# First cross attention of a decoder: another order of the short halves, of the turn and of the output copy, and the maxima split before they are turned

## The chip, the cores and the metric

The kernel runs on one core of a Trainium2 chip. The metric is the device time of one execution in microseconds; 706.71 us is the median of three runs of the kernel before (704.28 to 708.05).

## What is computed

A decoder of two layers over 4 sequences of 256 tokens with 128 channels: attention, cross attention to a context of 1601 tokens with 64 channels, a mixture of experts, a recurrent layer, a second cross attention and a feed-forward block, each with a residual and a layer norm. The change touches the first cross attention alone, which is a causal self attention and an attention to the context with the same 16 heads, added:

```python
def _xattn(x, cross_input):            # T=256, H=16 heads of D=8, scale 1/sqrt(8); 4 sequences
    q, k, v = heads(x @ Wq + bq), heads(x @ Wk + bk), heads(x @ Wv + bv)
    att = where(causal, einsum('bhqd,bhkd->bhqk', q, k) * scale, -inf)
    y = einsum('bhqk,bhkd->bhqd', softmax(att), v)
    qc = heads(x @ Wcq + bcq)
    kc, vc = heads(cross_input @ Wck + bck), heads(cross_input @ Wcv + bcv)
    attc = einsum('bhqd,bhkd->bhqk', qc, kc) * scale          # 1601 keys
    y = y + einsum('bhqk,bhkd->bhqd', softmax(attc), vc)
    return y @ Wp + bp
x = layernorm(x + attn(x)); x = layernorm(x + _xattn(x, ctx_512)); ...
```

The softmax is taken with the true maximum of each row subtracted.

## The kernel before

The first cross attention is cut into NU = 16 units, one for each sequence and group of four heads. The heads of a group lie as two pairs, e = 0 and 1, in rows 0 to 63 and 64 to 127 of TensorE's array; a pair holds heads j = 0 and 1. Queries and keys are split into three bf16 parts stacked over 48 rows, so that one bf16 product gives the scores to fp32 precision. Each unit is worked on twice:

- *Halves* (`score_part`, L692, and `reduce_half`, L1076) find the row maxima. A unit has HALVES = 15 of them: 12 of 512 keys (i = 0 to 11, VectorE reduces 2 x 512 columns, L1083), one with the last 65 keys of four query tiles (i = 12, L1085), and two for the self attention with its mask (i = 13 of 128 keys and i = 14 of 256, L1090). A half is written to two PSUM banks (`s1`), and there are two such pairs of banks, used in turn: a writer waits in `wait_s1_free` (L317) until what stood there two places earlier in the list `s1_order` has been read.
- After the last half `combine` (L1094) makes the negated maxima `nm` (128 x 16, fp32). TensorE turns them (`turn_maxima`, L723) to 16 rows of 128, in the place of `s1_order` between half 0 and half 1 of the next unit. VectorE's `row` (L1099) copies them to bf16 and subtracts the copy from the fp32 rows for the second part. SyncE then writes the two parts (`max_rows`, L374 to L381) as two more rows under the queries in `qq`, so that the second score product has its maximum subtracted. It is awaited as `max_in` before the first score product of that unit.
- *Score steps* (`scores_t`, L729): a unit has NST = 15, t = 0 to 12 for the context (128 keys each) and 13 and 14 for the self attention. Each gives four products (e, j) with the keys on the partitions; ScalarE takes exponentials of 512 columns for each e (L962), and `outputs` (L748) multiplies them with the values two steps later, into one bank `o_ps`. After a unit's last product ScalarE copies that bank to `o_all` (`copy_out`, L948), and the first product of the next unit waits for the copy. The scores `s2` have three banks (S2_RING), the exponentials four buffers (P_RING).

`scores_and_half` (L776) puts one score step and one half together in TensorE's queue, and the halves run S1_LEAD + HALVES = 22 steps ahead of the scores. So step g of the loop works on half (g + 22) mod 15 of a unit one or two ahead. 22 halves stand before the loop, in the start-up, and the last 22 score steps have no half beside them. Order and waits are written out by hand for every engine; semaphores count, and an engine's queue is strictly in order.

In TensorE's queue a step is: scores (0,0), half e = 1, scores (0,1), scores (1,0), half e = 0, scores (1,1), then, where i = 0, the turn, and then the four value products of the step before the last. Halves are counted by position i in the queue; VectorE follows in the same order. In ScalarE's queue the output copy of unit n - 1 stands behind both exponentials of step t = 1 of unit n.

## Time and profile before

| | us |
|---|---|
| median of 3 runs | 706.71 |
| lowest, highest | 704.28, 708.05 |
| the profiled execution | 703.72 |
| its span | 701.9 |
| PE, VectorE, ScalarE, GpSimd busy | 620.9, 527.3, 451.0, 205.6 |

The page gives shares and groups of one execution. The loop of the first cross attention runs from about 84 to 395 us of the span; an output copy (L950) marks every unit, the first at 108.7 and the last at 389.1. Times in the timelines are from the span's start. An entry such as "x8" merges eight instructions in a row, and its duration runs from the first's start to the last's end.

### The profile page before, as it was taken

How to read it: one execution, taken by the hardware profiler on the slowest of the kernel's cores; microseconds unless marked ns; L12 is line 12 of the kernel's file. 1: busy time of each engine (PE TensorE's matmuls, PEld its weight loads, DVE VectorE, ACT ScalarE, POOL GpSimd, SP SyncE). 2: the span in 40 equal slices, each digit the busy share in tenths (PEclk: the TensorE clock that was granted, in tenths of full speed). 3: DMA queues.
4: the chain of work that ended last, by engine and by line, in shares of the span. 5: the costliest groups of instructions: out<-in, count | busy, mean ns of one | idle time of the engine just before them, and what ended most of it. 6: DMA issues, size and time to landing. Idle time of an engine off the chain costs nothing. (4 is left out here: it accounts for less than half of the span.)

```text
span 701.9 us, 13641 instructions
## 1 busy us (share of the span) xinstructions
PE 620.9 (88%) x5206; PEld 341.4 (49%) x5207; DVE 527.3 (75%) x706; ACT 451.0 (64%) x814; POOL 205.6 (29%) x277
## 2 busy tenths in 40 slices
PE   8989899999999999999999796998709999978996
PEld 5645433333334333333433375886205556646883
DVE  5369889999999999999945464999298557868432
ACT  3555578888898888888887432655771056566223
POOL 7224532344455577766740030000000000005000
PEclk9999989999999999999999978999968999999998
DMA  8258575555565554544210287451000010000000
GB/s 204 95 148 267 172 227 173 140 116 138 161 157 121 124 138 98 116 96 97 66 36 1 70 299 312 151 166 59 0 2 0 0 46 1 1 1 1 0 1 30
DMA packets 43293, 70.74 MB, mean 101 GB/s; under 512 B 12492, under 2 KB 31652, under 8 KB 42720
## 3 DMA queue, kind: packets, MB, share of 16 engines
q1 hardware_dynamic: 31696, 38.34, 21.0%
q0 software_dynamic: 10928, 29.32, 13.5%
q10 hardware_dynamic: 608, 2.25, 1.4%
q8 instruction: 40, 0.66, 0.4%
q14 instruction: 21, 0.17, 0.1%
HBM read 44.41 MB, written 24.79 MB: 99 GB/s over the span
## 5 line engine op out<-in xcount | busy, mean ns | idle before, releaser
L962 ACT ACTIVATE prob<-ps 128x512 f32<-128x512 f32 (+2 forms) x480 | 253.1, 582 | 45.9 <-PE ps L738 38.8
L1083 DVE TENSOR_REDUCE pm<-ps 128x2 f32<-128x1024 f32 x192 | 225.8, 1215 | 6.6 <-PE ps L700 4.8
L761 PE MATMUL ps<-prob,vst 128*9 128x256 f32 (+1 forms) x1664 | 129.8, 384 | 10.2 <-ACT o_all L950 10.2
L738 PE MATMUL ps<-qq,kc 50*128 50x256 bf16 (+1 forms) x832 | 134.3, 275 | 0.1
L700 PE MATMUL ps<-kc,qq 48*128 48x512 bf16 x384 | 116.4, 388 | 2.9 <-DVE pm L1083 2.6
L738 PEld LDWEIGHTS ps<-qq,kc 50*128 50x128 bf16 (+1 forms) x832 | 52.1, 96 | 94.0 <-ACT prob L962 69.3
L761 PEld LDWEIGHTS ps<-prob,vst 128*9 128x9 f32 (+1 forms) x1664 | 25.1, 88 | 51.7 <-ACT prob L962 39.1
L1635 POOL DMA_DIRECT2D w_w<-in_w x2 | 1.1, 534 | 148.1 <-PE ps L1672 148.1
L1090 DVE TENSOR_REDUCE nm<-ps 128x4 f32<-128x512 f32 (+1 forms) x32 | 30.6, 958 | 14.9 <-PE ps L688 14.9
L700 PEld LDWEIGHTS ps<-kc,qq 48*128 48x128 bf16 x384 | 32.9, 93 | 13.2 <-DVE pm L1083 9.4
L688 PE MATMUL ps<-masks_b 64*128 64x256 bf16 x256 | 37.6, 269 | 0.0
L1663 PE MATMUL ps<-w_wgate 128*128 128x384 f32 x54 | 21.2, 540 | 17.2 <-DVE r_sn L2073 17.2
L1315 PE MATMUL ps<-x_high,up_high 128*128 128x512 f32 x64 | 26.6, 415 | 10.3 <-DVE hv L1483 6.4
L1394 ACT ACTIVATE sg<-ps,exp_bias 128x512 f32<-128x512 f32 x32 | 21.9, 685 | 17.3 <-PE ps L1317 17.2
L1399 ACT ACTIVATE hh_high<-whole 128x512 fp32r<-128x512 f32 x32 | 20.1, 627 | 19.7 <-DVE whole L1491 19.7
L1483 DVE SCALAR_TENSOR_TENSOR hv<-ps,exp_bias,sg 128x512 f32<-128x512 f32 x32 | 23.9, 746 | 9.5 <-DMA comb_bc<-comb_scr 7.5
L518 POOL TENSOR_TENSOR o_all<-o_all,below 128x512 f32<-128x512 f32 x13 | 16.5, 1271 | 48.4 <-DMA below<-rden_scr 48.4
L1989 ACT ACTIVATE ctx_t<-ps,base 128x512 f32<-128x512 f32 x16 | 11.0, 688 | 29.8 <-PE ps L1750 29.8
L1934 ACT ACTIVATE ps<-shift 128x512 f32<-128x512 f32 (+1 forms) x28 | 15.7, 569 | 21.4 <-DVE shift L2171 18.9
L1640 POOL TENSOR_TENSOR ctx<-ctx_t,ctx 128x512 fp32r<-128x512 f32 x4 | 5.2, 1292 | 72.9 <-DVE ctx L2230 72.9
L1317 PE MATMUL ps<-x_high,up_low 128*128 128x512 f32 x64 | 26.2, 410 | 0.0
L1316 PE MATMUL ps<-x_low,up_high 128*128 128x512 f32 x64 | 26.1, 408 | 0.0
(362 smaller groups left out, 1292.3 us busy)
## 6 DMA issues: line engine op xcount, KB each, us to landing
kc<-kc_scr SPq DMA_DIRECT2D x32, 300.2 KB, 5.0
comb_bc<-comb_scr SPq DMA_DIRECT2D x7, 512.0 KB, 4.7
below<-rden_scr POOLq DMA_DIRECT2D x13, 256.0 KB, 6.0
ctx<-ctx_scr POOLq DMA_DIRECT2D x1, 3204.0 KB, 15.0
raw<-in_wexp POOLq DMA_DIRECT2D x8, 384.0 KB, 3.9
exp_scr<-raw_high POOLq DMA_DIRECT2D x8, 384.0 KB, 3.5
exp_scr<-raw_low POOLq DMA_DIRECT2D x8, 384.0 KB, 4.4
kc_scr<-hi SPq DMA_DIRECT2D x6, 400.2 KB, 4.8
```

The costliest lines, as they stand in the source:

```text
L688: done = pe.matmul(o, ident_b[rows, half, :], mask[rows, half, :].unsqueeze(1).to_broadcast([64, 2, 128]), start=False, stop=(half == 1), ...
L700: return pe.matmul(bank, qq[s][rows, 0, j, t * 128:(t + 1) * 128], kc[s][rows, j, c * 512:(c + 1) * 512], start=True, stop=True)
L738: last = pe.matmul(bank[0:p, j * TQ:(j + 1) * TQ], kc[s][rows, j, t * 128:t * 128 + p], qq[s][rows, 0, j, :], start=(j == 0), stop=True, s ...
L761: last = pe.matmul(o_ps[32 * hh:32 * hh + VW, kind * TQ + q0:(kind + 1) * TQ], value[:, hh * VW:(hh + 1) * VW], prob[0:k, (NST * n + t) % ...
L962: act.activation(prob[0:p, g % P_RING, 2 * e:2 * e + 2, q0:TQ], s2[0:p, k % S2_RING, 0:2 * w].rearrange("p (i q) -> p i q", i=2), ACT.Exp, ...
L1083: dve.tensor_reduce(pm[:, m % 2, c, :, jt], banks, AX.X, ALU.max).then_inc(s1_read, 1)
L1090: dve.tensor_reduce(nm[:, :, 1, :].rearrange("p e (j t) -> p e j t", t=2)[:, :, :, t], banks[:, :, 0:2 * w].rearrange("p e (j n) -> p e j ...
L1315: pe.matmul(o, weight[0], x[0], start=start, stop=False, skip_group_check=True)
L1316: pe.matmul(o, weight[0], x[1], start=False, stop=False, skip_group_check=True)
L1317: return pe.matmul(o, weight[1], x[0], start=False, stop=True, skip_group_check=True)
L1394: act.activation(sg[:, k % 2, :], ps[:, k % 2, :], ACT.Silu, bias=exp_bias[s][:, f:f + 1]).then_inc(sg_done, 1)
L1483: dve.scalar_tensor_tensor(out=hv[:, k % 2, :], in0=ps[:, 2 + k % 2, :], scalar=exp_bias[s][:, NF + f:NF + f + 1], in1=sg[:, k % 2, :], op ...
```

## The change

- A table HALF_AT gives for each position in a unit which half is worked on there. From unit 2 on the order is 0, 1, 2, 12, 3, 4, 5, 13, 6, 7, 8, 14, 9, 10, 11; units 0 and 1 keep the old one. The wait for the self-attention queries goes with half 13.
- `turn_maxima` moves from the end of the step of half 0 into the step of half 1, behind both score products of e = 0 and ahead of the half. Its place in `s1_order` stays.
- The maxima are split on VectorE at once in `combine`: a cast of 128 x 16 to bf16 and a subtract, into `nm_parts`. The turn is then two bf16 matrix products with the identity, each 16 x 128, side by side in one bank. `row` leaves VectorE; ScalarE copies 16 x 256 in one instruction, behind both exponentials of the step of half 1.
- `copy_out` stands behind the first exponential of t = 1 and not behind the second.

```diff
@@ -51,6 +51,12 @@
 QPART = (0, 1, 2, 0, 1, 0)
 SLOTS = 4
 HALVES, TURN = 15, -1
+HALF_AT = (0, 1, 2, 12, 3, 4, 5, 13, 6, 7, 8, 14, 9, 10, 11)
+
+
+def half_at(m, i):
+    return HALF_AT[i] if m >= 2 else i
+
 P_RING, S2_RING = 4, 3
 S1_LEAD = 7
 WARM = 7
@@ -204,6 +210,7 @@
             vss = held(st, "vss", [128, NB, NG, 2, 4 * VW])
             pm = held(st, "pm", [128, 2, 4, 2, 4])
             nm = held(st, "nm", [128, 2, 2, 4])
+            nm_parts = held(st, "nm_parts", [128, 2, 16], BF16)
             mrow = [held(st, f"mrow{s}", [16, 2, 128], BF16) for s in range(SLOTS)]
             ps = st.enter_context(nc.psum_tensor("ps1", [128, 8, 512], F32))
             s1 = ps[:, 4:8, :].rearrange("p (n e) k -> p n e k", e=2)
@@ -691,7 +698,7 @@
 
                     def score_part(m, i, e):
 
-                        s, n = m % SLOTS, s1_at[m, i]
+                        s, n, i = m % SLOTS, s1_at[m, i], half_at(m, i)
                         bank = s1[:, n % 2, e, :]
                         rows = head_rows(e)
                         if i < 12:
@@ -716,7 +723,7 @@
                     def score_wait(m, i):
                         if i == 0:
                             pe.wait_ge(slot_in[m % SLOTS], SLOT_INC * (m // SLOTS + 1))
-                        if i == 13:
+                        if half_at(m, i) == 13:
                             pe.wait_ge(self_in[m % SLOTS], SELF_INC * (m // SLOTS + 1))
                         wait_s1_free(pe, s1_at[m, i])
 
@@ -724,7 +731,10 @@
                         n = s1_at[m, TURN]
                         wait_s1_free(pe, n)
                         pe.wait_ge(nm_ready, m + 1)
-                        pe.transpose(s1[0:16, n % 2, 0, 0:128], nm[:].rearrange("p e k i -> p (e k i)"), ident).then_inc(s1_ready, 1)
+                        for part in range(2):
+                            last = pe.matmul(s1[0:16, n % 2, 0, part * 128:(part + 1) * 128], nm_parts[:, part, :], ident_b[:, 0, :],
+                                             start=(part == 0), stop=True, skip_group_check=True)
+                        last.then_inc(s1_ready, 1)
 
                     def scores_t(n, t, e, j):
 
@@ -767,11 +777,11 @@
                     def half(h):
 
                         m, i = h // HALVES, h % HALVES
+                        if i == 1 and m:
+                            turn_maxima(m - 1)
                         score_wait(m, i)
                         score_part(m, i, 1)
                         score_part(m, i, 0).then_inc(s1_ready, 1)
-                        if i == 0 and m:
-                            turn_maxima(m - 1)
 
                     def scores_and_half(g, h):
 
@@ -781,18 +791,18 @@
                         m, i = h // HALVES, h % HALVES
                         more = m < NU
                         scores_t(n, t, 0, 0)
+                        if i == 1 and m <= NU:
+                            scores_t(n, t, 0, 1)
+                            turn_maxima(m - 1)
                         if more:
                             score_wait(m, i)
                             score_part(m, i, 1)
-                        scores_t(n, t, 0, 1)
+                        if i != 1 or m > NU:
+                            scores_t(n, t, 0, 1)
                         scores_t(n, t, 1, 0)
                         if more:
                             score_part(m, i, 0).then_inc(s1_ready, 1)
                         scores_t(n, t, 1, 1)
-                        if more and i == 0:
-                            turn_maxima(m - 1)
-                        if h == NU * HALVES:
-                            turn_maxima(NU - 1)
 
                     pe.wait_ge(masks_cast, 1)
                     for h in range(HALVES + S1_LEAD):
@@ -935,6 +945,12 @@
                     for j in range(5, LATE_KEYS):
                         middle(j - 1)
                         high(j)
+                    def row(m):
+                        n = s1_at[m, TURN]
+                        act.wait_ge(s1_ready, n + 1)
+                        act.activation(mrow[m % SLOTS][:].rearrange("p i n -> p (i n)"), s1[0:16, n % 2, 0, 0:256],
+                                       ACT.Copy).then_inc(mrow_ready, 1)
+
                     for h in range(HALVES + S1_LEAD):
                         if h == 0:
                             middle(LATE_KEYS - 1)
@@ -944,6 +960,8 @@
                             high(late_keys[h])
                         if h in late_values:
                             values(late_values[h])
+                        if h == HALVES + 1:
+                            row(0)
 
                     def copy_out(n):
                         act.wait_ge(av_done, NST * (n + 1))
@@ -962,8 +980,11 @@
                             act.activation(prob[0:p, g % P_RING, 2 * e:2 * e + 2, q0:TQ],
                                            s2[0:p, k % S2_RING, 0:2 * w].rearrange("p (i q) -> p i q", i=2),
                                            ACT.Exp, scale=SCALE).then_inc(exp_done, 1)
-                            if t == 1 and e == 1 and n:
+                            if t == 1 and e == 0 and n:
                                 copy_out(n - 1)
+                        m, i = divmod(g + HALVES + S1_LEAD, HALVES)
+                        if i == 1 and m <= NU:
+                            row(m - 1)
                     copy_out(NU - 1)
                     act_ln2a(0)
                     act_ln2a_v(0)
@@ -1075,7 +1096,7 @@
                         values(5 + i)
                     def reduce_half(m, i):
 
-                        n = s1_at[m, i]
+                        n, i = s1_at[m, i], half_at(m, i)
                         dve.wait_ge(s1_ready, n + 1)
                         banks = s1[:, n % 2, :, :]
                         if i < 12:
@@ -1094,15 +1115,14 @@
                     def combine(m):
                         dve.wait_ge(s1_read, HALVES * (m + 1))
                         dve.tensor_reduce(nm[:, :, 0, :], pm[:, m % 2].rearrange("p c e i -> p e i c"), AX.X, ALU.max,
-                                          negate=True).then_inc(nm_ready, 1)
-
-                    def row(m):
-                        n, u = s1_at[m, TURN], m % SLOTS
-                        dve.wait_ge(s1_ready, n + 1)
-                        dve.tensor_copy(mrow[u][:, 0, :], s1[0:16, n % 2, 0, 0:128]).then_inc(m1_done, 1)
-                        dve.wait_ge(m1_done, m + 1)
-                        dve.tensor_tensor(mrow[u][:, 1, :], s1[0:16, n % 2, 0, 0:128], mrow[u][:, 0, :],
-                                          ALU.subtract).then_inc(mrow_ready, 1)
+                                          negate=True).then_inc(m1_done, 1)
+                        whole = nm[:].rearrange("p e k i -> p (e k i)")
+                        dve.wait_ge(m1_done, 2 * m + 1)
+                        if m:
+                            dve.wait_ge(mrow_ready, m)
+                        dve.tensor_copy(nm_parts[:, 0, :], whole).then_inc(m1_done, 1)
+                        dve.wait_ge(m1_done, 2 * m + 2)
+                        dve.tensor_tensor(nm_parts[:, 1, :], whole, nm_parts[:, 0, :], ALU.subtract).then_inc(nm_ready, 1)
 
                     def reciprocals(n):
                         at = slice(n % 2 * DEN, (n % 2 + 1) * DEN)
@@ -1129,8 +1149,6 @@
                     for m in range(NU):
                         for i in range(HALVES):
                             reduce_half(m, i)
-                            if m and i == 0:
-                                row(m - 1)
                             if m >= 3 and i == 8:
                                 reciprocals(m - 3)
                             if m * HALVES + i in late_keys:
@@ -1139,7 +1157,6 @@
                                 dve.wait_ge(v_act, len(values_order) - DVE_VALUES)
                                 dve.memset(o_ps, 0.0).then_inc(o_zero, 1)
                         combine(m)
-                    row(NU - 1)
                     last_normalise(NU - 3)
                     projected(0)
                     last_normalise(NU - 2)
```

TensorE's queue around the turn of unit 1 (`nm`), before; `ps1` holds all banks, `qq0,kc0` are the score products of unit 0, `kc2,qq2` the halves of unit 2, `prob,vst` the value products:

```order
L738 MATMUL ps1<-qq0,kc0 128x256 [waits exp_done]
L700 MATMUL ps1<-kc2,qq2 128x512
L738 MATMUL ps1<-qq0,kc0 128x256
L727 MATMUL ps1<-base,nm 16x128 [waits nm_ready,s1_read]
L761 MATMUL ps1<-prob,vst 9x256 [waits exp_done]
L761 MATMUL ps1<-prob,vst 9x256 x3
L738 MATMUL ps1<-qq0,kc0 128x256 [waits exp_done]
L700 MATMUL ps1<-kc2,qq2 128x512 [waits s1_read]
L738 MATMUL ps1<-qq0,kc0 128x256
L738 MATMUL ps1<-qq0,kc0 128x256 [waits exp_done]
```

The same place in the changed kernel:

```order
L771 MATMUL ps1<-prob,vst 9x256 [waits exp_done]
L771 MATMUL ps1<-prob,vst 9x256 x3
L748 MATMUL ps1<-qq0,kc0 128x256 [waits exp_done]
L748 MATMUL ps1<-qq0,kc0 128x256
L735 MATMUL ps1<-masks_b,nm_parts 16x128 [waits nm_ready,s1_read]
L735 MATMUL ps1<-masks_b,nm_parts 16x128
L707 MATMUL ps1<-kc2,qq2 128x512 [waits s1_read]
L748 MATMUL ps1<-qq0,kc0 128x256 [waits exp_done]
L707 MATMUL ps1<-kc2,qq2 128x512
L748 MATMUL ps1<-qq0,kc0 128x256
L771 MATMUL ps1<-prob,vst 9x256 [waits exp_done]
L771 MATMUL ps1<-prob,vst 9x256 x3
```

The turn now stands between the score products of e = 0 and the half, one step later, and the score products of e = 1 stand behind the half.

VectorE's queue around it, before, from the short halves at the end of a unit to the rows' cast and subtract:

```order
L1085 TENSOR_REDUCE pm<-ps1 128x8 [waits s1_ready]
L1090 TENSOR_REDUCE nm<-ps1 128x2x2 [waits s1_ready] x2
L1096 TENSOR_REDUCE nm<-pm 128x2x4 [waits s1_read]
L1083 TENSOR_REDUCE pm<-ps1 128x2 [waits s1_ready]
L1102 CAST mrow1<-ps1 16x128 [waits s1_ready]
L1104 TENSOR_TENSOR mrow1<-ps1,mrow1 16x128 [waits m1_done]
```

and in the changed kernel:

```order
L1111 TENSOR_REDUCE nm<-ps1 128x2x2 [waits s1_ready]
L1104 TENSOR_REDUCE pm<-ps1 128x2 [waits s1_ready] x3
L1117 TENSOR_REDUCE nm<-pm 128x2x4 [waits s1_read]
L1123 CAST nm_parts<-nm 128x16 [waits mrow_ready,m1_done]
L1125 TENSOR_TENSOR nm_parts<-nm,nm_parts 128x16 [waits m1_done]
L1104 TENSOR_REDUCE pm<-ps1 128x2 [waits s1_ready] x3
```

The cast and the subtract have moved from behind the first reduction (L1083) of the next unit to ahead of it, and the masked half (L1090, now L1111) lies three plain reductions before the end.

ScalarE's queue at the step of half 1 in the changed kernel, where the kernel before has exponentials alone, and then at t = 1 of a unit, before and after:

```order
L980 ACTIVATE prob<-ps1 128x512 [waits s2_ready]
L980 ACTIVATE prob<-ps1 128x512 [waits s2_ready,av_done]
L980 ACTIVATE prob<-ps1 128x512 [waits s2_ready]
L951 ACTIVATE mrow3<-ps1 16x256 [waits s1_ready]
L980 ACTIVATE prob<-ps1 128x512 [waits s2_ready,av_done]
```

```order
L962 ACTIVATE prob<-ps1 128x512 [waits s2_ready]
L962 ACTIVATE prob<-ps1 128x512 [waits s2_ready,av_done]
L962 ACTIVATE prob<-ps1 128x512 [waits s2_ready]
L950 ACTIVATE o_all<-ps1 128x512 [waits av_done]
L962 ACTIVATE prob<-ps1 128x512 [waits s2_ready,av_done]
L962 ACTIVATE prob<-ps1 128x512 [waits s2_ready]
```

```order
L980 ACTIVATE prob<-ps1 128x512 [waits s2_ready]
L980 ACTIVATE prob<-ps1 128x512 [waits s2_ready,av_done]
L968 ACTIVATE o_all<-ps1 128x512 [waits av_done]
L980 ACTIVATE prob<-ps1 128x512 [waits s2_ready]
L980 ACTIVATE prob<-ps1 128x512 [waits s2_ready,av_done]
```

The row copy (L951) stands behind the exponentials of its step, and the output copy (L950, now L968) passes one exponential.

## Rows read from the trace of the kernel before

**Rows 1.** The page: span, busy, two groups (busy, mean ns | idle before).

```profile
span 701.9 us, 13641 instructions
...
PE 620.9 (88%) x5206; PEld 341.4 (49%) x5207; DVE 527.3 (75%) x706; ACT 451.0 (64%) x814; POOL 205.6 (29%) x277
...
L962 ACT ACTIVATE prob<-ps 128x512 f32<-128x512 f32 (+2 forms) x480 | 253.1, 582 | 45.9 <-PE ps L738 38.8
L1083 DVE TENSOR_REDUCE pm<-ps 128x2 f32<-128x1024 f32 x192 | 225.8, 1215 | 6.6 <-PE ps L700 4.8
```

**Rows 2.** Windows: stretch, us, busy time of each engine, clock, DMA share, GB/s.

```profile
202.00:221.00 19.00, 17.63 (x240) 7.22 (x237) 17.62 (x20) 16.56 (x33) 10.20 (x14) 1.00 0.62 149
```

**Rows 3.** Timeline, ScalarE: start, us, engine, line, operation [idle before <-releaser].

```profile
202.14 0.61 ACT L950 ACTIVATE o_all<-ps 128x512 f32<-128x512 f32 x1
...
211.84 4.35 ACT L962 ACTIVATE prob<-ps 128x512 f32<-128x512 f32 x8 [1.12 <-PE ps L738]
...
220.80 0.61 ACT L950 ACTIVATE o_all<-ps 128x512 f32<-128x512 f32 x1
```

**Rows 4.** Timeline, VectorE, around the end of a unit's halves.

```profile
207.38 0.69 DVE L1090 TENSOR_REDUCE nm<-ps 128x4 f32<-128x512 f32 x1 [0.34 <-PE ps L688]
208.70 1.23 DVE L1090 TENSOR_REDUCE nm<-ps 128x4 f32<-128x1024 f32 x1 [0.62 <-PE ps L688]
209.96 0.21 DVE L1096 TENSOR_REDUCE nm<-pm 128x8 f32<-128x32 f32 x1
210.08 1.22 DVE L1083 TENSOR_REDUCE pm<-ps 128x2 f32<-128x1024 f32 x1
211.21 0.27 DVE L1102 CAST mrow<-ps 16x128 bf16<-16x128 f32 x1
211.51 0.28 DVE L1104 TENSOR_TENSOR mrow<-ps,mrow 16x128 bf16<-16x128 f32 x1
211.90 9.39 DVE L1083 TENSOR_REDUCE pm<-ps 128x2 f32<-128x1024 f32 x8
```

**Rows 5.** TensorE: steps, turn, halves 1 and 2, awaited product.

```profile
207.83 0.28 PE L738 MATMUL ps<-qq,kc 50*128 50x256 bf16 x1
...
209.14 0.28 PE L738 MATMUL ps<-qq,kc 50*128 50x256 bf16 x1
...
210.31 0.27 PE L727 MATMUL ps<-base,nm 128*16 128x128 f32 x1 [0.56 <-DVE nm L1096]
...
211.35 0.39 PE L700 MATMUL ps<-kc,qq 48*128 48x512 bf16 x1
...
212.44 0.39 PE L700 MATMUL ps<-kc,qq 48*128 48x512 bf16 x1
...
213.53 0.28 PE L738 MATMUL ps<-qq,kc 50*128 50x256 bf16 x1
...
218.24 0.28 PE L738 MATMUL ps<-qq,kc 50*128 50x256 bf16 x1
...
221.55 0.62 PE L761 MATMUL ps<-prob,vst 128*9 128x256 f32 x8 [0.68 <-ACT o_all L950]
```

**Rows 6.** Waits, window 110 to 370: who waited for whom: us, times, longest.

```profile
PEld ps L727 <- DVE nm L1090: 11.5, 14, 1.0
PE ps L761 <- ACT o_all L950: 9.5, 14, 0.7
```

**Rows 7.** SyncE timeline, and GB/s over 211 to 218 us.

```profile
211.82 2.74 SPq L380 DMA_DIRECT2D qq<-mrow  x4
...
GB/s 94 94 54 7 0 0 0 0 0 0 0 0 12 0 0 0 12 0 0 0 12 0 0 0 12 0 220 203 256 73 183 366 335 237 79 116 262 116 146 329
```

**Rows 8.** Timelines, small operations on ScalarE and VectorE.

```profile
79.96 0.52 ACT L898 ACTIVATE vst<-ps 128x432 f32<-128x432 f32 x1
80.34 0.22 DVE L1004 TENSOR_TENSOR rem<-ps,hi 128x65 f32<-128x65 f32 x1
83.92 0.29 ACT L898 ACTIVATE vst<-ps 65x144 f32<-65x144 f32 x1 [0.18 <-PE ps L582]
```

## The prediction

> **What bounds the kernel now.** I read the page first: TensorE (PE) is busy 88% of the span and the two costliest groups are ScalarE's exponentials (L962) and VectorE's maxima (L1083) [rows 1]. Busy shares don't name a limit here, so I took the table of windows. In one stretch of 19.00 us in the middle of the cross attention PE is busy 17.63, VectorE 17.62 and ScalarE 16.56 [rows 2]: three engines within 1.1 us of each other, at the full clock. What counts is then the waits that they pass on to one another, and I read the timeline of each engine over one unit.
>
> The output copy (L950), once in each unit, gives the period: it starts at 202.14 and 220.80 [rows 3], 18.66 us for 15 steps. A step without anything special takes PE 1.09 us (212.44 to 213.53) [rows 5], ScalarE 1.09 (8 exponentials in 4.35 us, two to a step) [rows 3] and VectorE about 1.17 (8 reductions in 9.39) [rows 4]. 15 plain steps of 1.09 would be 16.35, so 2.3 us of the period are extras: mask steps (the step from 207.83 to 209.14 takes 1.31 [rows 5], there are four, one of them with a shorter product behind it), the turn of the maxima, and the wait of the first product of a unit for the output copy, 0.68 at 221.55 [rows 5], 9.5 us over 14 units [rows 6].
>
> The turn is the largest. VectorE starts its last reduction of a unit at 208.70 and ends at 209.93. Call this end R. It combines (209.96, 0.21), reduces the first half of the next unit (210.08, 1.22, end 211.30), then casts and subtracts the turned rows (211.21, 211.51; they are ready at 211.79) [rows 4]. PE turns at 210.31, starts half 1 of the next unit at 211.35, as soon as half 0 has been read (R + 1.42), and half 2 at 212.44 (R + 2.51) [rows 5]. ScalarE is idle 1.12 us before 211.84 for it [rows 3], and PE's weight load for the turn waits 11.5 us over 14 units [rows 6].
>
> **The change, part by part.**
>
> *The turn and the split.* Halves and the turn share two buffers in turn. Order: half 0, turn, half 1, half 2. So half 1 waits until half 0 has been read, and half 2 until the turned rows have been copied. Neither rule is changed, but what stands ahead of both gets longer.
>
> Step one, VectorE. The combine is followed by a cast and a subtract of 128x16, each waiting for the one before. The trace has no such operation. The nearest are the combine, 0.21 for 32 elements to 8 [rows 4], and a subtract of 65 columns from PSUM, 0.22 [rows 8]; the ends are 0.10 and the 0.28 of the subtract of 128 columns [rows 4]. I take 0.18 each, a little under the 65-column one. With the 0.03 us between dependent ones (209.93 to 209.96, 211.48 to 211.51) and the 0.09 by which an independent reduction starts ahead of its predecessor's end (210.08 against 210.17) the reduction of half 0 starts at R + 0.03 + 0.21 + 2 x (0.03 + 0.18) - 0.09 = R + 0.57 and ends at R + 1.79; it ended at R + 1.37. PE gets to half 1 at R + 1.84, 0.42 later than now.
>
> Step two, PE. Before, the wait for the maxima stood behind all score products of step 0. Now the turn stands inside step 1, ahead of half 1, and the scores of the second head pair (e = 1) stand behind half 1's first part. They can't start before R + 1.84. From the start of half 1's first part to their results is 0.23 + 0.11 + 0.27 = 0.61 us (the product L738 is 0.28 long [rows 5]; the other two are half a half's columns and one product's columns, as the 1.09-step spaces them). The exponential starts at about R + 2.49.
>
> Step three, ScalarE. The row copy stands behind that exponential, so it starts one exponential later (4.35 / 8 = 0.54): R + 3.03. Its price: the copies of 144 and 432 columns took 0.29 and 0.52 [rows 8], so 256 columns are near 0.38, with these two as ends. Rows ready at R + 3.41, half 2 on PE at R + 3.45 instead of R + 2.51: **+0.94 us** per unit. With 0.10 or 0.28 for the two split operations it is +0.78 or +1.14. The two casts from PSUM that VectorE loses (0.27 + 0.28) [rows 4] give nothing back, since they ran while VectorE waited for half 1 anyway (211.35 + 0.55 = 211.90).
>
> The Trainium skill (VectorE: DVE Perf Modes, "The TRN2 errata") gives two prices that differ for the small operations: 58 + FD cycles for SBUF to SBUF, which would be 0.08 us, and (N + 151)/0.96 ns for an fp32 tensor_tensor, 0.17 us. By the first the turn would cost +0.74 instead of +0.94, by the second it stays. This trace shows nothing under 0.2 us on VectorE [rows 4, 8], so it leans to the second.
>
> *Short steps.* A 4 x 65-column half and the two self-attention halves move from the end of the unit to places 3, 7 and 11, for all units but the first two. Instructions and durations stay. The last half is then a plain one. Start of step to start of reduction was 0.87 for the masked one (207.83 to 208.70) and is 0.55 for a plain one (211.35 to 211.90) [rows 4, 5]: -0.32. The mask step's extra of 1.31 - 1.09 = 0.22 now lies ahead of it: +0.22. Together **-0.10**. That VectorE no longer idles through three short halves in a row is worth nothing as long as PE and ScalarE set the pace between turns, and with 1.09 against their 1.09 they do.
>
> *Output copy.* It is queued one exponential earlier, so the first product's wait of 0.68 [rows 5] shrinks by 0.54, at most. The exponential it passes is later by the copy's own place in the queue (0.61 long [rows 3]), and the product behind needs that one. Gain between 0 and 0.54; I take the middle, **-0.30**.
>
> *Knock-on.* ScalarE has 0.3 us more work per unit and enters half 2 with two waits (before e = 1 and before the next step) in place of one. It is busy 16.56 of 19.00 [rows 2], so it can catch up, but only at PE's pace. 0 to 0.3, I take **+0.15**.
>
> Sum: 0.94 - 0.10 - 0.30 + 0.15 = **+0.69 us** per unit, the ends 0.78 - 0.10 - 0.54 = +0.14 and 1.14 - 0.10 + 0.3 = +1.34. It is paid where a turn is followed by halves of the next unit in the steady loop: turns 1 to 14, so 14 x 0.69 = +9.7 (ends +2 and +19). Turn 0 lies in the start-up, turn 15 has no half behind it; the last unit wins the copy's 0.3. These cancel. The profiled execution is at 703.7 (span 701.9 [rows 1] and 1.8 around it), 3 us below the median of 706.7; the sum is put on the median: 716.5.
>
> **The rivals.**
>
> *The rows reach the next unit too late.* SyncE issues four small transfers in 2.74 us from 211.82 [rows 7] and the next unit's first scores start at 218.24 [rows 5], 6.45 us after the rows were ready. The rows are now ready at R + 3.41 instead of R + 1.86, 1.55 later, and everything behind is 0.94 later: 5.8 us are left. The line of bytes over 211 to 218 us shows four equal pulses of 12 GB/s, the last one 24 slices of 0.175 us in, at 215.2 [rows 7]: 3.4 to 3.6 us after the rows. So some 2 us of margin. If loads of experts or of keys fall on these transfers (the same line stands at 200 and more right behind them) and it takes 7 us, each unit pays 1.2 more: 716.5 + 14 x 1.2 = 733. Chance 0.08, and half of that price in some units is likelier than all of it.
> The Trainium skill (DMA: Bandwidth & Descriptors, the table of fixed and variable cost) says some 2.0 us for one transfer; behind three issues of about 0.7 that makes 4.1 us, inside the 5.8 as well.
>
> *Faster: VectorE's queue was the bound.* The change was then worth what VectorE idles now. Its own work after it would be 12 plain halves x 1.17, two of 128 and 65 columns at 0.69 less the 0.08 of overlap, 1.20 for the longer masked one and 0.57 for combine and split [rows 4]: 14.04 + 1.22 + 1.20 + 0.57 = 17.0 us, and 0.55 for the one half that nothing covers (between half 0 and half 1 VectorE has no rows to split any more): 17.6 per unit, 1.1 below 18.66, and 706.7 - 15 = 692. It decides if, at the turn, half 0 has been read before PE comes to half 1. For it: three short halves in a row now leave VectorE idle, and spread out they let it catch up, since 1.17 against 1.09 means that it falls behind in long rows. Against it: the chain R to half 2 is made of waits that the order of the code forces, however early R is, and moving R earlier by an idle time of VectorE needs PE to deliver earlier. Chance 0.14, with anything from 692 to 703.
>
> *No difference.* The chain is at its low end and the copy's gain at its high end: +0.14 x 14 = +2, 703 to 710. Chance 0.12.
>
> **How the numbers follow.** Forecast (711 to 723, likeliest 716.5) 0.66, late rows 0.08, same 0.12, faster 0.14. A measurement of this kernel can tell about 0.5%, 3.5 us, from no change. Slower by more: 0.66 + 0.08 = 0.74; within: 0.12; faster: 0.14. The range leaves out the faster case and the top of the late one: 703 to 724.
>
> **What would show it.** In the profile of the changed kernel: the output copies 19.3 us apart in place of 18.66; before one exponential in each unit an idle time of ScalarE above 1 us with a second one behind it; PE's first half product waiting for VectorE's maxima once in a unit, and once for ScalarE's row copy, which did not exist; the wait of the first value product for the output copy near 0.15. If the copies are 17.6 apart and PE waits for neither, step two is wrong. If the first scores of a unit wait for the rows' transfer, the first rival holds. If the split operations take 0.1 each or less, the size is wrong, by 0.2 us per unit.

## The result, and the profile after

The changed kernel takes 728.7 us, the median of four runs (722.8 to 734.0), against 705.5 us for the kernel before beside it: a ratio of 1.031, 95% interval 1.026 to 1.037. It was forecast slower, 716.5 with a range to 724, so the sign was right and the size was not: +23 us in place of +10. One of the four executions, 722.8, lies inside the range. Executions more than 1.5% above the fastest of the same kernel, here 734.0, are left out of every ratio but not out of the medians. The profiled execution took 729.7, with a span of 727.9.

The page of the changed kernel, the lines that answer to [rows 1]; PEclk is the granted clock in 40 slices, in tenths:

```profile
span 727.9 us, 13704 instructions
...
PE 643.0 (88%) x5222; PEld 344.3 (47%) x5223; DVE 528.5 (73%) x706; ACT 455.0 (63%) x830; POOL 205.7 (28%) x277
...
PEclk9999789989999999999999998899967999999999
...
L980 ACT ACTIVATE prob<-ps 128x512 f32<-128x512 f32 (+2 forms) x480 | 252.2, 584 | 63.0 <-PE ps L748 55.1
L1104 DVE TENSOR_REDUCE pm<-ps 128x2 f32<-128x1024 f32 x192 | 230.2, 1218 | 37.1 <-PE ps L707 35.9
```

The busy times of VectorE and ScalarE have hardly moved, but VectorE's idle time ahead of its reductions went from 6.6 to 37.1 us and ScalarE's ahead of its exponentials from 45.9 to 63.0. TensorE (PE) is busy 22 us longer with 16 instructions more: something made the same products take longer.

The output copies mark the units. In ScalarE's timeline of the changed kernel four of them stand here:

```profile
175.47 0.60 ACT L968 ACTIVATE o_all<-ps 128x512 f32<-128x512 f32 x1
...
194.79 0.60 ACT L968 ACTIVATE o_all<-ps 128x512 f32<-128x512 f32 x1
...
215.57 0.60 ACT L968 ACTIVATE o_all<-ps 128x512 f32<-128x512 f32 x1
...
236.39 0.60 ACT L968 ACTIVATE o_all<-ps 128x512 f32<-128x512 f32 x1
```

They are 19.32, 20.78 and 20.82 us apart, where [rows 3] had 18.66. Of the first 13 distances six lie between 19.32 and 19.57 and seven between 20.78 and 22.24. The kernel before has 18.66 to 18.78 for all 13. So there are two losses, one in every unit and one in about half of them.

**The first loss is the chain of the turn.** VectorE's timeline in the changed kernel around one turn:

```profile
220.08 3.48 DVE L1104 TENSOR_REDUCE pm<-ps 128x2 f32<-128x1024 f32 x3
223.59 0.21 DVE L1117 TENSOR_REDUCE nm<-pm 128x8 f32<-128x32 f32 x1
223.83 0.17 DVE L1123 CAST nm_parts<-nm 128x16 bf16<-128x16 f32 x1
224.04 0.17 DVE L1125 TENSOR_TENSOR nm_parts<-nm,nm_parts 128x16 bf16<-128x16 f32 x1
224.13 1.22 DVE L1104 TENSOR_REDUCE pm<-ps 128x2 f32<-128x1024 f32 x1
```

ScalarE's at the same turn:

```profile
226.05 0.60 ACT L980 ACTIVATE prob<-ps 128x512 f32<-128x512 f32 x1 [1.22 <-PE ps L748]
226.55 0.36 ACT L951 ACTIVATE mrow<-ps 16x256 bf16<-16x256 f32 x1
227.62 1.08 ACT L980 ACTIVATE prob<-ps 128x512 f32<-128x512 f32 x2 [0.71 <-PE ps L748]
```

And TensorE's:

```profile
223.76 0.39 PE L748 MATMUL ps<-qq,kc 50*128 50x256 bf16 x2
224.36 0.27 PE L735 MATMUL ps<-masks_b,nm_parts 128*16 128x128 bf16 x2 [0.22 <-DVE nm_parts L1125]
225.41 0.39 PE L707 MATMUL ps<-kc,qq 48*128 48x512 bf16 x2 [0.78 <-DVE pm L1104]
...
226.96 0.55 PE L707 MATMUL ps<-kc,qq 48*128 48x512 bf16 x1 [0.18 <-ACT mrow L951]
```

The last reduction of the unit ends at 223.56; this is R. Half 1 starts at R + 1.85, the exponential of e = 1 at R + 2.49 after 1.22 us of idle time, the rows are ready at R + 3.35 and half 2 starts at R + 3.40. In the kernel before it was R + 2.51 [rows 4, 5].

**The second loss is TensorE's clock.** The windows of 2 us behind this turn (stretch, us, busy time of PE, PEld, DVE, ACT, POOL, granted clock, DMA share, GB/s):

```profile
224.00:226.00 2.00, 1.01 (x12) 0.38 (x14) 1.37 (x4) 0.84 (x2) 1.81 (x4) 1.00 0.09 17
226.00:228.00 2.00, 1.82 (x19) 0.54 (x22) 1.41 (x2) 1.24 (x3) 0.00 (x0) 0.76 0.65 197
228.00:230.00 2.00, 2.00 (x26) 0.73 (x20) 1.30 (x2) 1.16 (x3) 1.43 (x2) 0.50 0.02 3
230.00:232.00 2.00, 2.00 (x29) 0.78 (x23) 1.20 (x2) 1.58 (x4) 1.70 (x2) 0.88 0.67 157
```

PE was busy half of the window at the turn. Then the granted clock falls to 0.50, which is 1.2 GHz in place of 2.4, and comes back 3.4 us later (227.0 to 230.5). The windows of the kernel before showed the full clock in mid-loop [rows 2].

The waits of the changed kernel in its loop, 110 to 390 us:

```profile
PE ps L707 <- DVE pm L1104: 10.1, 13, 0.8
...
PE ps L735 <- DVE nm_parts L1125: 4.0, 13, 1.1
...
PE ps L771 <- ACT o_all L968: 3.0, 14, 0.2
PE ps L707 <- ACT mrow L951: 2.2, 12, 0.2
...
PEld ps L748 <- DMA qq<-mrow: 0.4, 1, 0.4
```

The wait for the output copy, 9.5 us in [rows 6], is 3.0; the waits for the row copy are new, those for half 0 go from 0.2 us at the most to 0.8; the rows' transfers made nobody wait but once.

**The books.** From the profile of before (701.9) to that of after (727.9) are 26.0 us. The first output copy stands at 113.1 instead of 108.7: 4.4. The first 13 distances sum to 263.9 against 13 x 18.68 = 242.8: 21.1, of which 13 x (19.33 - 18.68) = 8.5 is the chain and 12.6 stands on top, 12.3 of it in the seven longer units. Not all of that is the clock: in two of the seven a split operation on VectorE was held up, 1.0 us together (see "The clock"). The last two distances gained 0.6, and behind the last copy 1.1 came on top. Which units are hit differs from one to the next and the medians cover several executions, so the 12.6 is this execution's.

### The profile page after: what moved, and what is told of

It is laid out like the page before. It is cut to its first block and busy times, and to the rows that moved or that the text cites. A ratio compares the mean times of both kernels' runs of the same rounds, so it can differ in the third digit from the quotient of the medians.

```text
span 727.9 us, 13704 instructions
## 1 busy us (share of the span) xinstructions
PE 643.0 (88%) x5222; PEld 344.3 (47%) x5223; DVE 528.5 (73%) x706; ACT 455.0 (63%) x830; POOL 205.7 (28%) x277
## 5 line engine op out<-in xcount | busy, mean ns | idle before, releaser
L1104 DVE TENSOR_REDUCE pm<-ps 128x2 f32<-128x1024 f32 x192 | 230.2, 1218 | 37.1 <-PE ps L707 35.9
L748 PE MATMUL ps<-qq,kc 50*128 50x256 bf16 (+1 forms) x832 | 143.1, 283 | 0.4 <-ACT vst L908 0.2
L771 PE MATMUL ps<-prob,vst 128*9 128x256 f32 (+1 forms) x1664 | 136.3, 401 | 3.2 <-ACT o_all L968 3.2
L707 PE MATMUL ps<-kc,qq 48*128 48x512 bf16 x384 | 118.7, 401 | 17.3 <-DVE pm L1104 14.0
L748 PEld LDWEIGHTS ps<-qq,kc 50*128 50x128 bf16 (+1 forms) x832 | 55.1, 97 | 105.4 <-ACT prob L980 75.3
L1416 ACT ACTIVATE hh_high<-whole 128x512 fp32r<-128x512 f32 x32 | 20.1, 627 | 21.5 <-DVE whole L1508 21.5
L1111 DVE TENSOR_REDUCE nm<-ps 128x4 f32<-128x512 f32 (+1 forms) x32 | 30.7, 958 | 2.6 <-PE ps L695 1.4
L1951 ACT ACTIVATE ps<-shift 128x512 f32<-128x512 f32 (+1 forms) x28 | 15.7, 569 | 21.4 <-DVE shift L2188 18.9
L509 POOL DMA_DIRECT2D below<-o_all x13 | 9.2, 707 | 70.1 <-ACT o_all L968 70.1
```

The lines of the kernel that those rows point to most:

```text
L707: return pe.matmul(bank, qq[s][rows, 0, j, t * 128:(t + 1) * 128], kc[s][rows, j, c * 512:(c + 1) * 512], start=True, stop=True)
L748: last = pe.matmul(bank[0:p, j * TQ:(j + 1) * TQ], kc[s][rows, j, t * 128:t * 128 + p], qq[s][rows, 0, j, :], start=(j == 0), stop=True, s ...
L771: last = pe.matmul(o_ps[32 * hh:32 * hh + VW, kind * TQ + q0:(kind + 1) * TQ], value[:, hh * VW:(hh + 1) * VW], prob[0:k, (NST * n + t) % ...
L1104: dve.tensor_reduce(pm[:, m % 2, c, :, jt], banks, AX.X, ALU.max).then_inc(s1_read, 1)
L1111: dve.tensor_reduce(nm[:, :, 1, :].rearrange("p e (j t) -> p e j t", t=2)[:, :, :, t], banks[:, :, 0:2 * w].rearrange("p e (j n) -> p e j ...
```

## The experiments

Each was measured beside the kernel before on the same chip. "At full clock" below is the distance that recurs among the first 13 output copies. The mean granted clock is that of the windows from 114 to 352 us.

### One part at a time

`order_only` is the kernel before with the new places of the short halves, `copy_only` with the earlier output copy, `turn_only` the changed kernel without these two:

```diff
--- order_only against the kernel before (and half_at(m, i) where a half is written and reduced)
+HALF_AT = (0, 1, 2, 12, 3, 4, 5, 13, 6, 7, 8, 14, 9, 10, 11)
--- copy_only against the kernel before
-                            if t == 1 and e == 1 and n:
+                            if t == 1 and e == 0 and n:
--- turn_only against the changed kernel
-HALF_AT = (0, 1, 2, 12, 3, 4, 5, 13, 6, 7, 8, 14, 9, 10, 11)
+HALF_AT = tuple(range(15))
-                            if t == 1 and e == 0 and n:
+                            if t == 1 and e == 1 and n:
```

> The kernel before with the new places of the short halves alone. The two traces say that the turn costs what was lost (output copies 19.33 us apart in the units at full clock, 18.67 before) and that TensorE's clock then falls to half after some of the turns (20.8 apart). Theory A, the turn: the order of halves moves no wait of the turn, so +0 to +0.15 us per unit, 704 to 709. Rival, the order of halves: with plain halves at the end VectorE arrives later at the turn, at least a third of the 22 us comes from it: 713 or more.

> The kernel before with the output copy one exponential earlier, alone. The first value product of a unit waited 0.68 us for it. Theory A: the wait falls to 0.15 to 0.2 and some of it comes back elsewhere, -0.15 to -0.3 us per unit, 701 to 704. Rival: the exponential that it passes is late by as much, no change, 706.

> The changed kernel with the old order of the halves and the old place of the output copy: the split, the bf16 turn inside the step of half 1 and ScalarE's row copy are left. Theory A (turn and clock carry all of the loss, and the copy's own gain of 0.34 us per unit is inside the changed kernel's time): copies 19.4 to 19.7 apart at full clock, half clock after some turns, 727 to 735. Rival (loss comes from the combination with the order of halves): under 722.

| kernel | us | ratio to before (95%) | copies apart at full clock | mean clock |
|---|---|---|---|---|
| order_only | 707.2 | 1.004 (1.001 to 1.006) | 18.78 | 1.00 |
| copy_only | 699.9 | 0.992 (0.989 to 0.995) | 18.33 | 1.00 |
| turn_only | 736.2 | 1.045 (1.039 to 1.051) | 19.56 | 0.94 |
| the change | 728.7 | 1.031 (1.026 to 1.037) | 19.33 | 0.95 |

Against 18.67 the parts are +0.11, -0.34 and +0.89 us per unit. Their sum, +0.66, is the distance of the whole change, 19.33: at full clock the parts add up. The output copy is a gain by itself and the turn is the loss, together with all of the half clock. The rivals of all three expectations fall. Theory A holds for the distances; two times lie outside their ranges, `copy_only` 1.1 us below and `turn_only` 1.2 above.

### The clock

`fill3` gives TensorE three products without use behind the turn, while it waits for half 0 to be read. Nobody reads them.

```diff
                         last.then_inc(s1_ready, 1)
+                        constant = masks_b[:].rearrange("p i h n -> p (i h n)")
+                        for _ in range(3):
+                            pe.matmul(s1[:, n % 2, 1, :], constant[:, 0:128], constant[:, 0:512], start=True, stop=True)
```

> The changed kernel with three matrix products of 512 columns without use behind each turn, written to the bank beside the turned rows, so that TensorE has work while it waits for VectorE to read half 0 (0.78 us in the trace). Theory A, the clock falls because TensorE stands idle at the turn: no unit at half clock, all output copies 19.3 to 19.4 apart, 716 to 719. Rival, the clock falls for another reason (or the idle time is not what decides): 726 to 731, and the copies 20.8 apart as often as now.

Measured: 715.2 us, 1.017 (1.011 to 1.023), 0.8 us below the expected range, and below the changed kernel by 13 us with 48 products more. The window of 114 to 352 us, of the kernel before:

```profile
114.00:352.00 238.00, 222.03 (x3013) 91.72 (x3005) 220.52 (x243) 206.31 (x396) 134.96 (x192) 1.00 0.51 120
```

Of the changed kernel:

```profile
114.00:352.00 238.00, 221.29 (x2794) 86.51 (x2790) 204.78 (x224) 193.57 (x377) 124.78 (x175) 0.95 0.47 117
```

Of `fill3`:

```profile
114.00:352.00 238.00, 226.92 (x2930) 90.28 (x2939) 213.47 (x235) 200.60 (x392) 129.57 (x183) 1.00 0.48 118
```

The mean clock is back at 1.00. Eleven of the 13 distances are 19.32 to 19.37; two are 19.90 and 19.99, at full clock, for a reason of their own (below). The first output copy stands at 108.2, where the kernel before has it, so the 4.4 us of the start-up go away with the filling too. That the clock falls because TensorE stands idle at the turn is shown by this: nothing else was changed, and the chain of 19.33 is untouched. The length of a wait alone doesn't decide: in the start-up of `fill3` TensorE waits 0.88 and 0.94 us in one piece (before 80.5 and 88.7 us), and the clock stays full.

**A third effect: the split is sometimes held up.** This is what lengthened the two units of `fill3`. GpSimd's and VectorE's timelines there:

```profile
134.73 1.81 POOL L480 TENSOR_TENSOR raw_low<-raw,raw_high 128x768 fp32r<-128x768 f32 x1
135.81 0.76 DVE L1126 CAST nm_parts<-nm 128x16 bf16<-128x16 f32 x1
```

The cast takes 0.76 us in place of 0.17 and ends 0.03 us after GpSimd's operation. In the traces of the seven kernels that split the maxima in SBUF, 26 of 224 casts and subtracts take 0.31 to 1.44 us, and each of the 26 ends 0.03 to 0.04 us after a cast or tensor_tensor of GpSimd. In the seven kernels that read the turned rows from PSUM, the same two operations take 0.27 and 0.28 us all 224 times. This is read from the traces; no experiment tested it. The changed kernel has two of the 26 (a subtract of 0.31 and a cast of 1.03), `turn_only` five, `fill3` two, `e1_first` three, `e1_fill` six, `turn_end` and `row_between` four each. In the five kernels without filling all 18 turns with such an operation are followed by half clock, of the 52 other turns of the loop nine.

### Step two: the scores of e = 1 behind the half

`e1_first` sends the score products of e = 1 ahead of half 1 in the step of the turn; `e1_fill` is the same with two products without use ahead of the turn and two ahead of half 1.

```diff
                             scores_t(n, t, 0, 1)
                             turn_maxima(m - 1)
+                            scores_t(n, t, 1, 0)
+                            scores_t(n, t, 1, 1)
                         if more:
                             score_wait(m, i)
                             score_part(m, i, 1)
```

> The changed kernel with the score products of e = 1 ahead of the half in the step of the turn, so that ScalarE's second exponential and the row copy behind it don't wait for VectorE to read half 0. Split, bf16 turn and row copy on ScalarE stay. Theory A (step two of the chain, the scores of e = 1 queued behind the half): rows ready about 1.2 us earlier, half 2 no longer waits for them, 18.6 to 18.9 us per unit, TensorE's idle time shorter and the clock held: 706 to 711. Rival (the split on VectorE and the row copy themselves are the price): 716 or more.

> The run with the score products of e = 1 ahead of the half, and on top two products without use between the slot's release and the turn and two between those scores and half 1. That run had units of 18.65 us at full clock and of 20.4 to 20.6 with half clock. Theory A (idle time at the turn lowers the clock): all units at 18.65 to 18.8, 704 to 708, no difference to the kernel before. Rival: the clock falls as often, 711 to 715.

`e1_first`: 713.4 us, 1.012 (1.005 to 1.020). At full clock the copies are 18.64 to 18.71 apart, one 18.90. That is 0.68 us of each unit back with the split, the bf16 turn and ScalarE's row copy in place. It is the distance of the kernel before, but the other two parts are in it too: 18.67 + 0.11 - 0.34 = 18.44, so of the turn's 0.89 us 0.21 are left. ScalarE's timeline at an ordinary turn, idle 0.15 in place of 1.22 before the exponential in front of the row copy:

```profile
258.24 0.60 ACT L985 ACTIVATE prob<-ps 128x512 f32<-128x512 f32 x1 [0.15 <-PE ps L748]
258.74 0.36 ACT L956 ACTIVATE mrow<-ps 16x256 bf16<-16x256 f32 x1
```

TensorE is idle 0.22 us before that turn and 0.46 before half 1:

```profile
257.61 0.27 PE L735 MATMUL ps<-masks_b,nm_parts 128*16 128x128 bf16 x2 [0.22 <-DVE nm_parts L1130]
...
258.66 0.39 PE L707 MATMUL ps<-kc,qq 48*128 48x512 bf16 x2 [0.46 <-DVE pm L1109]
```

No ordinary turn of the loop, eleven in all, is followed by half clock. The other three are those where GpSimd held the cast up (0.45, 0.55 and 0.62 us long); the first wait is then 0.50 to 0.67, and the three distances are 20.4 to 20.6. One such stretch in the windows:

```profile
198.00:200.00 2.00, 1.27 (x14) 0.45 (x14) 1.51 (x3) 1.21 (x3) 1.71 (x3) 0.99 0.00 0
200.00:202.00 2.00, 2.00 (x22) 0.56 (x14) 1.56 (x2) 0.94 (x2) 1.65 (x4) 0.50 0.11 19
```

So the distance was forecast rightly and the time, 706 to 711, was not: the clock was not held in every unit.

`e1_fill`: 709.6 us, 1.007 (1.004 to 1.010), no unit at half clock (mean clock 1.00), though six split operations are held up. Eight of its copies are 18.9 apart and not 18.65, the five others 19.0 to 19.6: four products are more than the gap holds, and each unit pays 0.27 us for them. So it comes out 1.6 us above the expected range. The traced execution, 714.5, is the slowest of its ten.

### The place of the turn and of the row copy

`turn_end` puts the turn back to the end of the step of half 0 and the row copy behind that step's exponentials. `row_between` leaves the turn and puts the row copy between the two exponentials of its step.

```diff
--- turn_end against the changed kernel (scores_and_half; half and the row copy go with it)
-                        if i == 1 and m <= NU:
-                            scores_t(n, t, 0, 1)
-                            turn_maxima(m - 1)
...
                         scores_t(n, t, 1, 1)
+                        if i == 0 and m <= NU:
+                            turn_maxima(m - 1)
--- row_between against the changed kernel, inside the loop over e
+                            m, i = divmod(g + HALVES + S1_LEAD, HALVES)
+                            if e == 0 and i == 1 and m <= NU:
+                                row(m - 1)
```

> The changed kernel with the turn back at the end of the step of half 0, behind all of its score products, and the row copy behind that step's exponentials. The split on VectorE ahead of half 0's reduction and the copy on ScalarE stay. Theory A: the chain is then 0.4 us longer than before the change (the split) and no longer 0.9, TensorE's idle time is cut in two by the turn: copies 18.8 to 19.0 apart, clock mostly held, 708 to 714. Rival (not the place of the turn but the split and the row copy): 19.3 and more, above 716.

> The changed kernel with ScalarE's row copy between the two exponentials of its step in place of behind them; nothing else. Theory A, step three: the row copy no longer waits for the exponential of e = 1, whose scores stand behind half 1; half 2 waits for the rows no more, copies 18.8 to 18.9 apart at full clock against 19.33. TensorE's idle time of 0.78 us before half 1 stays, and so do the units at half clock: 718 to 723. Rival (the place of the row copy is nothing, the wait for half 0's reduction is all): 19.3 apart, 726 to 731.

`turn_end`: 711.6 us, 1.008 (1.004 to 1.011), copies 18.86 apart at full clock. With the turn where it was, the split and the row copy cost 18.86 - 18.44 = 0.42 us per unit, 18.44 being 18.67 with the two other parts (+0.11 - 0.34), and the other 0.47 of the turn's 0.89 are its new place, with the row copy's. The time lies in the expected range. The traced execution, 721.6, does not stand for it: of eleven executions four, this one among them, took 718 to 723 and seven 706 to 713. In it five of the 13 distances are 20.4 to 22.6, four of them at turns where a split operation was held up. At an ordinary turn TensorE waits longer in one piece than in the changed kernel, and one of ten such turns, not this one, was followed by half clock:

```profile
198.17 0.22 PE L735 MATMUL ps<-masks_b,nm_parts 128*16 128x128 bf16 x1 [1.09 <-DVE nm_parts L1123]
```

`row_between`: 718.8 us, 1.018 (1.011 to 1.024), seven copies 18.86 to 18.94 apart at full clock, one 19.12 and five 20.4 to 22.7, four of these five with a split operation held up. ScalarE's timeline:

```profile
215.32 0.36 ACT L951 ACTIVATE mrow<-ps 16x256 bf16<-16x256 f32 x1
216.64 0.60 ACT L980 ACTIVATE prob<-ps 128x512 f32<-128x512 f32 x1 [0.96 <-PE ps L748]
```

The row copy now runs 1.3 us before the exponential that it used to stand behind, and 19.33 - 18.87 = 0.46 us of each unit are saved by exchanging two entries of one queue. The exponential of e = 1 is as late as ever; only half 2 doesn't wait for it through the row copy. Both expectations of distance are met, and both kernels, whose gaps at the turn were left open, show half clock after five of 14 turns.

### Shortening the chain

If the time of a unit follows the two reductions around the turn, they should be short ones. `best1` is the kernel before with the earlier output copy and halves ordered for that: the 65-column half first, the 128-key half last. `pool_early` is the kernel before with GpSimd's broadcast of the reciprocals issued before its splits; `best2` has both, and `best3` also a later place for VectorE's reciprocals.

```diff
--- best1 against the kernel before (with half_at as above, and the wait for the self-attention data at the first of its two halves)
+HALF_AT = (12, 0, 1, 2, 3, 4, 5, 6, 7, 14, 8, 9, 10, 11, 13)
-                            if t == 1 and e == 1 and n:
+                            if t == 1 and e == 0 and n:
--- pool_early against the kernel before, best2 against best1
                                 gather(n - 2)
+                        if 1 <= n <= POOL_UNITS:
+                            reciprocals_back(n - 1)
...
                                 split_slab(i)
-                        if 1 <= n <= POOL_UNITS:
-                            reciprocals_back(n - 1)
--- best3 against best2
-                            if m >= 3 and i == 8:
+                            if m >= 3 and i == 12:
```

> The kernel before with the output copy one exponential earlier and another order of halves from unit 2 on: the 4 x 65-column half first, the 128-key self half last, the 256-key one in the tenth place; turn, cast and subtract as before. Theory A says that the time of a unit follows the chain of two reductions around the turn (last half, then half 0): with 0.69 in place of 1.23 and 1.22 it is 1.1 us shorter, and VectorE keeps pace between turns: copies 17.5 to 17.8 apart against 18.67, 686 to 692. Rival (the sum of VectorE's work is the bound, whatever the order): 18.2 to 18.3 as with the earlier copy alone, 698 to 701.

> The kernel before with GpSimd issuing the transfer that broadcasts the reciprocals before it splits experts and context, not after. GpSimd waited 48 us for that transfer in the window of the loop, but nothing waits for GpSimd while a unit takes 18.67 us. So no difference: 702 to 706, copies 18.67 apart. It is the control for the next two.

> The last run of the eight before (the 65-column half first, the 128-key half last, earlier output copy), whose copies stood 17.42 us apart but in four units 19 to 24, where VectorE waited up to 3.4 us for the denominators that GpSimd sends; with the broadcast issued before GpSimd's splits. Theory: GpSimd's cycle of 19 to 20 us falls below 17.4, no such wait, all units at 17.4: 686 to 690. Rival: GpSimd is not what is late, 695 to 698.

> As the run before, and VectorE takes the reciprocals behind its thirteenth half of a unit in place of the ninth, 4.4 us later, so that late denominators meet no wait. Theory: if the earlier broadcast alone is enough, the same time as without it, within 2 us; if some denominators are still late, 1 to 4 us less.

| kernel | us | ratio to before (95%) | copies apart |
|---|---|---|---|
| best1 | 696.5 | 0.989 (0.984 to 0.994) | 17.42, four of 17.9 to 23.9 |
| pool_early | 705.2 | 1.000 (0.998 to 1.003) | 18.67 |
| best2 | 686.3 | 0.973 (0.968 to 0.979) | 17.41 to 17.54, all 13 |
| best3 | 687.8 | 0.974 (0.969 to 0.980) | 17.51, one of 19.8 and one of 17.9 |

`best1` came out 0.1 us under its distance, 17.42, and missed its time. Its rival, that VectorE's work is the bound in any order, is refuted by the distance; what was missing is a third party. In two units VectorE waited for the denominators that GpSimd sends, and GpSimd for its own broadcast; VectorE's timeline in `best1`:

```profile
308.29 0.25 DVE L1118 RECIPROCAL below<-below 128x16 f32<-128x16 f32 x1 [3.37 <-DMA below<-o_all]
```

Two lines of its waits, 110 to 370 us:

```profile
POOL o_all L524 <- DMA below<-rden_scr: 60.6, 12, 7.4
...
DVE below L1118 <- DMA below<-o_all: 5.0, 2, 3.4
```

From one transfer of the denominators to the next GpSimd takes 20.0 us on the mean in `best1` between 161 and 321 us, so it falls behind units of 17.42. In the kernel before, three rounds of 19.8 to 21.5 are followed by shorter ones, and VectorE never waited for them. TensorE also waited three times, up to 2.0 us, for the rows' transfer, which is what the prediction's first rival described. In `best2` the first of these waits is

```profile
POOL o_all L524 <- DMA below<-rden_scr: 4.6, 1, 4.6
```

and the second is gone. The same edit alone changes nothing (`pool_early`), as a wait on an engine that nobody waits for should not. VectorE around the turn in `best2`:

```profile
202.39 0.68 DVE L1096 TENSOR_REDUCE nm<-ps 128x4 f32<-128x512 f32 x1
203.10 0.20 DVE L1102 TENSOR_REDUCE nm<-pm 128x8 f32<-128x32 f32 x1
203.32 0.70 DVE L1091 TENSOR_REDUCE pm<-ps 128x8 f32<-128x520 f32 x1
203.94 0.27 DVE L1108 CAST mrow<-ps 16x128 bf16<-16x128 f32 x1
204.24 0.28 DVE L1110 TENSOR_TENSOR mrow<-ps,mrow 16x128 bf16<-16x128 f32 x1
204.85 9.29 DVE L1089 TENSOR_REDUCE pm<-ps 128x2 f32<-128x1024 f32 x8 [0.33 <-PE ps L706]
```

TensorE's at the same turn:

```profile
203.46 0.27 PE L733 MATMUL ps<-base,nm 128*16 128x128 f32 x1 [0.16 <-DVE nm L1102]
...
204.21 0.28 PE L744 MATMUL ps<-qq,kc 50*128 50x256 bf16 x1
...
205.30 0.28 PE L744 MATMUL ps<-qq,kc 50*128 50x256 bf16 x1
```

Here the 0.91 us between 17.42 and `copy_only`'s 18.33 can be counted. TensorE waits 0.16 for the maxima and not 0.56: 0.40. Half 0 has been read when TensorE comes to half 1, so that step takes 1.09 (204.21 to 205.30) and not the 1.38 of `copy_only` (209.54 to 210.92): 0.29. And the wait for the output copy, 0.21 in `copy_only`, is gone. Which of the three moved halves brought how much was not taken apart. `best3` is no better than `best2`. Its units are 17.51 apart, and in the one of 19.8 TensorE waited 1.32 us for the rows' transfer and ran 3.4 us at half clock.

## Why the prediction was wrong

The direction and the chain of the turn were right. The step that failed is the sum: it took the chain's length as the whole price and put TensorE's clock at full, so the half clock behind the turn's waits had no term. The time lay 4.7 us above the range.

- **What bounds the kernel.** Three engines nearly level, so that waits passed on at the turn decide: held. The rival that VectorE's queue is the bound asked for units of 17.6 us and for no wait of TensorE; they took 19.33, with both waits.
- **The split.** 0.18 us for each operation, measured 0.17 where GpSimd doesn't hold it up; half 1 at R + 1.84, measured R + 1.85. That an operation between two SBUF tiles could be held up by GpSimd had no term either: 1.0 us in this trace. Of the two figures in the Trainium skill (VectorE: DVE Perf Modes, "The TRN2 errata") the one for an fp32 tensor_tensor, (N + 151)/0.96 ns, gives 0.174 for 16 columns, and the trace agrees; 58 + FD cycles (the table's 58 + FD/Accel with Accel at 1), 0.08, is half of what was measured.
- **Steps two and three.** Exponential at R + 2.49, measured R + 2.49; row copy 0.38, measured 0.36; half 2 at R + 3.45, measured R + 3.40. The price of the turn, +0.94 per unit, is +0.89 in `turn_only`. `e1_first` and `row_between` show each link apart: 0.68 and 0.46 us come back.
- **Short steps.** -0.10 forecast, +0.11 measured in `order_only`: the wrong sign. The step let a plain last reduction start 0.55 us behind its step on TensorE. In `order_only` VectorE reduces without a pause up to the end of the unit, one start every 1.13 us against TensorE's 1.09, and the last reduction starts 0.77 behind its step (207.20 to 207.97). With 0.22 more, -0.10 becomes +0.12.
- **Output copy.** -0.30 forecast, -0.34 measured in `copy_only`. The wait was to be near 0.15 and is 3.0 / 14 = 0.21.
- **Knock-on.** +0.15 forecast. None shows at full clock: `turn_only` holds chain and knock-on, forecast +1.09 together, and costs 0.89, which is how much later half 2 starts (R + 3.40 against R + 2.51).
- **The sum.** +0.69 per unit forecast, +0.66 measured, 19.35 against 19.33 us between copies. That it is so close is partly luck: 0.21 too little for the short steps stands against 0.24 too much for turn, output copy and knock-on. It was multiplied by 14 and called the whole. With the clock held the kernel does take 715.2 (`fill3`), next to the likeliest 716.5.
- **The missing term.** The working read the clock as full from one row of the kernel before [rows 2] and carried it over. The same waits that it priced at 0.94 us leave TensorE idle 0.22 and 0.78 us around a turn that is itself 0.27 long and short of work, and in seven of 13 units the clock was at 0.50 for 3.4 us afterwards, in one for 6.8: some 11.3 us in the loop (the 12.3 of the seven units without the 1.0 of the split), and 4.4 before the first copy. `fill3` took both back. The row that should have warned was in the trace before: the granted clock of the start-up, where PE waits 0.41 to 0.66 us for halves to be read (85 to 88 us), was below full already there (0.93 in the window of 90 to 114 us).
- **The first rival** (late rows) did not come: 0.4 us in all. The last of the rows' packets ran 3.5 us after the rows were ready (230.4 against 226.91), inside the 5.8 us. The Trainium skill (DMA: Bandwidth & Descriptors, "Anatomy of one DMA — SWDGE (gpsimd) path") gives a fixed 2.0 us for a transfer that GpSimd issues; these are SyncE's, and the trace has their first packets 1.3 us behind the issue (226.93, 228.25).

What stays open is why, of twelve turns of the changed kernel without a held split, five are followed by half clock and the others, most with the same gap to 0.01 us, are not, and so how many units an execution loses.

## What to carry to other kernels

Price a wait on TensorE twice: by its length, and by what the clock does after it. Where a change opens a gap of about a microsecond in a loop that ran with half of one, put a case with half clock behind it into the range. When three engines are level, look at which entries of each queue stand behind the one that waits: moving score products ahead of a waiting half, or one small copy ahead of an exponential, changed a unit by 0.5 to 0.7 us with the work unchanged, and choosing the shortest work for both sides of the one point where all engines wait for each other gave 0.91 us of 18.33; with the earlier output copy and broadcast the kernel is 2.7% faster. When a bound is lifted by 1 us per round, check the round of every engine that seemed free. And when a small operation on a chain moves from PSUM to SBUF, look at its longest duration and not only at its median.

## What was not expected of the hardware

- The granted clock fell to 0.50 after idle times of about 1.0 us in two pieces (five of twelve ordinary turns of the changed kernel, one of ten in `row_between`), 0.89 in two (two of nine in `turn_only`), 1.09 in one (one of ten in `turn_end`) and 0.95 to 1.13 in two (three of three in `e1_first`). It stayed full at all turns of the loop with 0.56 us in one piece (the kernel before), 0.67 in one (`order_only`) and 0.68 in two (`e1_first`).
- A cast of 16 columns between two SBUF tiles took up to 1.37 us in place of 0.17, and each time that it took over 0.3 it ended with an operation of GpSimd.
- 48 products without use made a kernel 13 us faster.
- In the changed kernel ScalarE took 0.357 us, all 16 times, for a copy of 256 columns on 16 partitions, 0.02 below what the interpolation from 65- and 128-partition copies [rows 8] gives: few partitions made it hardly shorter.
